# First chunks of every fold taken out of the rank-2 projection and put into w2

## The chip, the cores and the metric

One core of a Trainium2 chip runs the kernel. The metric is the device time in microseconds of one execution; the median of three runs before the change is 841.76 us (841.53 to 842.29). The engines are named as the profile names them: PE (matmul), DVE (VectorE), ACT (ScalarE), POOL (GpSimd) and SP, which issues the DMAs.

## What is computed

The input x has 2 x 2048 rows of 1024. Each row is normalised (xn); g is a gated feed-forward network with rank-2 additions to its three weights, and s an aggregation over lags of the row's autocorrelation:

```python
def _qlora_linear(x, wq, A, B):
    w = jnp.tile(wq, (1, 4))
    return x @ w.T + (x @ A.T @ B.T) * 0.5

xn = _layernorm(x)
s  = _L0_attn_ref(xn)              # sum over the 6 strongest lags, softmax weights
gate = silu(_qlora_linear(xn, w1q, a1, b1))
up   = _qlora_linear(xn, w3q, a3, b3)
g  = silu(_qlora_linear(gate * up, w2q, a2, b2))
return x + s * g
```

The weights are tiled four times along their inputs, so products with them are taken of a folded input: four quarters are added first. With gate * up = h (2752 wide), the last product is fold(h) @ w2q.T plus half of (h @ a2.T) @ b2.T, where a2 is 2 x 2752.

## The kernel before

The 4096 rows are taken in eight **token groups** of 512 (i = 0 to 7). In a token group the 2752 hidden columns are taken as 22 **pairs** p (a gate and an up matmul chain each, `up(i, p)`), ordered so that pairs 4n to 4n+3 are the four quarters of fold chunk n (n = 0 to 4), and pairs 20 and 21 hold what is left over, the rests. An even pair is a chain of six matmuls for gate and six for up, an odd one begins with `lora` (four matmuls of 32 rows that close the pair before and open this one). ACT makes silu of gate (`gate`), DVE multiplies with up (`product`, into one of six slots of h) and adds the quarters of a fold (`add_chunk`). Each folded chunk is split into a high part (ACT, `folded_high`) and a low part (DVE, `folded_low`, tile hf_l), and `down` multiplies both with w2, itself split into w2_h (ACT, `w2_high`) and w2_l (DVE, `w2_low`, `w2_tail`). In token group 0 `down` is split into `down_high` and `down_low`, since w2_l is still being made.

The rank-2 projection of h by a2 is `z2`: a **batch** is four pairs, each a matmul that gives 6 rows of 512 in a strip of the bank zb. `Z2_AT` says after which pair a batch stands, and the last one stands in the down projection. For fold chunks 3 and 4 (`BASE`) the first quarter is in no batch: a2 of the quarter is subtracted from that of the three others (POOL, `a2_diff`), and its outer product with b2, halved, is added to w2 by DVE, two rank-1 steps `add_base` per chunk with the rows of b2 broadcast by DMA (base_b). So 20 of 22 pairs stand in five batches. In the tail, `tail_shifts` (ACT) and `tail_sums` (DVE) move and add the strips of pairs 20 and 21.

Token group 0 has work that the others don't have: the split of the weights (`w_high`, `w_low`, with w_low ahead of the first chain of a weight block at pairs 4, 10 and 16), of b (`b_step`), of w2, and the x of token group 1 is transposed (`second_x`, four of its eight behind pairs 14 to 17; the first of those waits until `lag_gap` on DVE has reduced the bank mb). POOL computes the inverse deviations (`spread`) and the sums and differences of xn (`sums`: yh, xq, dd) of the next token group, four tiles per group. The order of each engine's work is written by hand: tables such as `BASE_AT`, `W2_AT`, `NORM_AT` and `STATS_AT` name the pair after which a step stands. DMAs are all issued by SP in the order of its program.

## Time and profile before

| what | value |
|---|---|
| median of three runs | 841.76 us |
| the profiled execution | 841.59 us |
| its span, first to last instruction | 839.8 us |
| PE busy | 821.7 us (98%) |
| DVE busy | 583.8 us (70%) |
| ACT busy | 331.6 us (39%) |
| POOL busy | 148.4 us (18%) |
| granted TensorE clock | full in all 40 slices |
| chain that ended last | PE 87%, DVE 5%, ACT 3% |

Matmuls overlap in the trace: each is shown with its whole duration, and the next starts before it has ended; the distance of two starts is what one costs. The shares are means over stages that differ: DVE's 70% is 97% from 47 to 74 us and less in the token groups behind.

### The profile page before, as it was taken

The page shows a single profiled execution, that of the slowest core. Times are in us where ns is not written, and L with a number is a line of the kernel's source. Part 1 is how long each engine was busy: PE and PEld are TensorE (multiplying, and loading weights), DVE is VectorE, ACT ScalarE, POOL GpSimd, SP SyncE. Part 2 cuts the span into 40 slices and gives each one's busy share as a digit, 9 for nine tenths or more (in the row PEclk, how much of TensorE's full clock was granted, in tenths as well). Part 3 has the DMA queues.
Part 4 walks back from the last instruction along what each step waited for, and adds up shares of the span by engine and source line. Part 5 has one row for each costly group of instructions (what it writes and reads, how often), then busy time and mean ns, then how long its engine had stood idle before and what let it go on. Part 6 is the DMA issues. An engine that isn't in the chain of part 4 may idle for free.

```text
span 839.8 us, 11191 instructions
## 1 busy us (share of the span) xinstructions
PE 821.7 (98%) x4168; PEld 438.9 (52%) x4168; DVE 583.8 (70%) x947; ACT 331.6 (39%) x544; POOL 148.4 (18%) x242
## 2 busy tenths in 40 slices
PE   5999999999999999999999999999999999999997
PEld 4444575345844367434763347534585345844366
DVE  7889844686766876688667785678776696744535
ACT  5986644434133342333423432333423434132231
POOL 5324102222012220122102230023201222000000
PEclk9999999999999999999999999999999999999999
DMA  9832035000230003300051010501015000220004
GB/s 286 291 96 76 26 123 204 26 26 25 102 126 26 26 26 126 101 26 26 27 176 50 26 51 2 201 25 51 26 52 176 26 0 1 101 101 1 0 2 151
DMA packets 19191, 63.18 MB, mean 75 GB/s; under 512 B 2496, under 2 KB 4256, under 8 KB 18864
## 3 DMA queue, kind: packets, MB, share of 16 engines
q1 hardware_dynamic: 19120, 62.33, 21.6%
q8 instruction: 33, 0.54, 0.3%
q14 instruction: 38, 0.31, 0.1%
HBM read 45.54 MB, written 16.78 MB: 74 GB/s over the span
## 4 chain that ended last, share of the span: by engine, by line
PE 87%; DVE 5%; ACT 3%; issue 2%; DVEq 2%; DMA 1%; SPq 0%; POOL 0%; ACTq 0%; POOLq 0%
PE g L1290 26%; PE u L1290 23%; PE g L1508 4%; PE u L1508 4%; PE zb L1449 4%; PE u L1517 4%; PE g L1517 4%; PE u L1515 4%; PE g L1515 4%; PE g L1341 3%; ACT w_sq L567 1%; PE mb L1378 1%; DMA xf<-in_x 1%; PE g L1511 1%; PE u L1511 1%
## 5 line engine op out<-in xcount | busy, mean ns | idle before, releaser
L567 ACT ACTIVATE sil<-g,winv 128x512 f32<-128x512 f32 (+1 forms) x176 | 119.9, 683 | 269.2 <-PE g L1341 240.3
L889 DVE SCALAR_TENSOR_TENSOR h<-u,winv,sil 128x512 f32<-128x512 f32 x168 | 125.6, 749 | 113.0 <-ACT sil L567 97.6
L1290 PE MATMUL g<-xt,w_h 128*128 128x512 f16 x656 | 196.2, 381 | 0.0
L1290 PE MATMUL u<-xt,w_h 128*128 128x512 f16 x656 | 195.1, 379 | 0.0
L832 DVE CUSTOM_DVE_ANT_0 junk<-xn,abc 128x1024 bf16<-128x1024 f32 x96 | 120.3, 1253 | 6.0 <-issue 2.7
L1290 PE MATMUL u<-xt,w_l 128*128 128x512 f16 x328 | 124.3, 379 | 0.0
L1290 PE MATMUL g<-xt,w_l 128*128 128x512 f16 x328 | 124.3, 379 | 0.0
L1290 PEld LDWEIGHTS u<-xt,w_h 128*128 128x128 f16 x656 | 64.2, 98 | 77.4
L1290 PEld LDWEIGHTS g<-xt,w_h 128*128 128x128 f16 x656 | 55.4, 98 | 83.9 <-issue 33.3
L464 POOL TENSOR_TENSOR ve<-mv,three 128x1 f32<-128x1 f32 x30 | 6.2, 207 | 471.7 <-DVE mv L814 471.7
L1040 DVE SCALAR_TENSOR_TENSOR ob<-xr,c_mean,gg 128x1024 f32<-128x1024 f32 x27 | 34.6, 1283 | 58.1 <-ACT gg L567 35.4
L567 ACT ACTIVATE gg<-g 128x512 f32<-128x512 f32 x32 | 19.1, 598 | 140.5 <-PE g L1511 65.9
L1508 PE MATMUL g<-w_h,hf_h 128*128 128x512 f32 x174 | 71.6, 411 | 1.4 <-ACT gg L567 1.4
L1508 PE MATMUL u<-w_h,hf_h 128*128 128x512 f32 x174 | 69.0, 397 | 0.0
L1517 PE MATMUL u<-w_h,hf_l 128*128 128x512 f32 x145 | 57.5, 397 | 0.0
L1517 PE MATMUL g<-w_h,hf_l 128*128 128x512 f32 x145 | 57.4, 396 | 0.0
L1515 PE MATMUL u<-w_l,hf_h 128*128 128x512 f32 x145 | 57.4, 396 | 0.0
L1515 PE MATMUL g<-w_l,hf_h 128*128 128x512 f32 x145 | 57.4, 396 | 0.0
L901 DVE TENSOR_TENSOR acc<-acc,h 128x512 f32<-128x512 f32 x80 | 57.1, 714 | 0.0
L1290 PEld LDWEIGHTS g<-xt,w_l 128*128 128x128 f16 x328 | 32.1, 98 | 38.7
L1290 PEld LDWEIGHTS u<-xt,w_l 128*128 128x128 f16 x328 | 32.1, 98 | 38.7
L511 POOL TENSOR_TENSOR yh<-xn 128x512 f32<-128x512 f32 x28 | 37.1, 1324 | 46.9 <-ACT xn L567 46.9
(258 smaller groups left out, 1138.2 us busy)
## 6 DMA issues: line engine op xcount, KB each, us to landing
xr<-in_x SPq DMA_DIRECT2D x32, 512.0 KB, 4.6
out_x<-ob SPq DMA_DIRECT2D x31, 512.0 KB, 2.9
xf<-in_x SPq DMA_DIRECT2D x30, 512.0 KB, 3.3
raw_w<-in_w2t SPq DMA_DIRECT2D x1, 2560.0 KB
abc<-in_a SPq DMA_DIRECT2D x1, 2048.0 KB, 8.1
raw_w<-in_w1t SPq DMA_DIRECT2D x2, 768.0 KB, 8.4
raw_w<-in_w3t SPq DMA_DIRECT2D x2, 768.0 KB, 9.8
base_b<-in_w2t SPq DMA_DIRECT2D x2, 512.0 KB, 4.8
```

Of the source, the lines that this page charges most:

```text
L511: tt(yh[:], xn[:, 0:HALF], xn[:, HALF:L], ALU.add).then_inc(sum_done, 1)
L567: return nc.scalar.activation(out, in_, f, **kw)
L832: nc.vector.tensor_tensor_reduce(junk[:], xn[:], abc[:, r, :], 1.0, 0.0, ALU.mult, ALU.add, zt[:, q, r:r + 1]).then_inc(z_done, 1)
L889: stt(out=h[0:n, p % NH, :], in0=up, scalar=winv[0:n, 3 * block_of(p) + 1:3 * block_of(p) + 2], in1=sil[0:n, p % 2, :], op0=ALU.mult, op1= ...
L901: o = tt(acc[0:rows, b, :], a, h[0:rows, p % NH, :], ALU.add)
L1040: stt(out=o[:], in0=x[:], scalar=c_mean[:, q:q + 1], in1=gg[:], op0=ALU.subtract, op1=ALU.mult)
L1290: o = mm(bank[:], a, x, start=opens and t == 0, stop=closes and t == len(terms) - 1)
L1341: o = mm((gb, ub)[s % 2][k % 3][:], bst[32 * s:32 * s + 32, p // 2, :], zst[32 * s:32 * s + 32, :], start=s >= 2 and not first, stop=s < 2 ...
L1449: o = mm(zb[c:c + 6, :], a2st[:, p, :], h[:, p % NH, :], start=n == 0, stop=n == ZB - 1)
L1508: mm(bank[:], hf_h[:, n, t], w2_h[:, n, c:c + 512], start=n == 0, stop=False)
L1515: mm(bank[:], hf_h[:, n, t], w2_l[:, n, c:c + 512], start=False, stop=False)
L1517: mm(bank[:], hf_l[:, n, t], w2_h[:, n, c:c + 512], start=False, stop=False)
```

## The change

All five fold chunks, and the rests, now have their first part in w2. In the rests pair 20 and the strip of pair 21 are brought together in one projection (`JOINT`): a copy by ACT puts the upper half of pair 21 over the lower rows of pair 20's slot. 16 pairs are left, in four batches, at other pairs of the order. The first rank-1 step per chunk of w2 is now a multiplication by ACT (`base_share`, two buffers share0 and share1) and an addition by POOL (`add_share`); the second stays with DVE (`add_base`), six instead of two, with a row of b2 of its own (base_b1). `w2_high` waits for it in all six chunks.

```diff
-BASE = (3, 4)
-Z_PAIRS = tuple(p for p in range(NP_) if p not in [4 * n for n in BASE])
+NBASE = HN + 1
+JOINT = 4 * HN
+Z_PAIRS = tuple(p for p in range(JOINT) if p % 4) + (JOINT,)
...
-        W2L_AT = {19: 0, 20: 1}
...
-        BASE_AT = {10: (0, 0), 12: (1, 0), 17: (0, 1), 18: (1, 1)}
-        Z2_AT = {5: 0, 9: 1, 13: 2, 19: 3}
+        SHARE_AT = {8: 0, 9: 1, 12: 2, 13: 3, 15: 4, 17: 5}
+        SHARE_BEHIND = ((0,), (), (3, 4), (5,))
+        BASE_AT = {10: 0, 16: 1, 17: 2, 18: 3, 19: 4, 20: 5}
+        C_LOADS = 13
+        Z2_AT = {7: 0, 12: 1, 17: 2}
...
-        W2_AT = {13: 0, 15: 1, 16: 2, 19: 3, 20: 4, 21: 5}
+        W2_AT = {13: 0, 17: 1, 18: 2, 19: 3, 20: 4, 21: 5}
...
+                    if i == 0:
+                        sp.wait_ge(b_rest_done, 4)
+                        sp.dma_start(base_b1[:], d["w2t"][97, HN, :].partition_broadcast(P)).then_inc(base1_loaded, 16)
                     front_load(i + 1, 3)
...
+            def add_share(n):
+                pool.wait_ge(w2_loaded, 16 * 7)
+                pool.wait_ge(share_done, n + 1)
+                tt(raw_w2[:, n, :], raw_w2[:, n, :], share[n % 2][:], ALU.add).then_inc(share_added, 1)
...
                     if i + 1 < NG:
                         spread(i + 1, q)
+                        if i == 0 and q in (1, 2):
+                            add_share(q)
                         sums(i + 1, q)
+                        if i == 0:
+                            for n in SHARE_BEHIND[q]:
+                                add_share(n)
...
-                A(half_b[0:32, :], h[32:64, LAST % NH, :], ACT.Copy).then_inc(shift_done, 1)
-                act.wait_ge(half_done, at_group(i, 2, 2))
+                act.wait_ge(half_done, at_group(i, 2, 1))
+                A(h[0:32, JOINT % NH, :], h[32:64, LAST % NH, :], ACT.Copy).then_inc(shift_done, 1)
                 A(half_b[0:32, :], half_a[32:64, :], ACT.Copy).then_inc(shift_done, 1)
+
+            def base_share(n):
+                act.wait_ge(base_loaded, 16)
+                act.wait_ge(base_halved, HN + 1)
+                if n >= 2:
+                    act.wait_ge(share_added, n - 1)
+                A(share[n % 2][:], base_b[:], ACT.Copy, scale=base_a[:, n, 0:1]).then_inc(share_done, 1)
...
-                if n in BASE:
-                    act.wait_ge(base_done, 2 + BASE.index(n) + 1)
+                act.wait_ge(base_done, n + 1)
...
+            def add_base(n):
+                dve.wait_ge(share_added, n + 1)
+                dve.wait_ge(base1_loaded, 16)
+                stt(out=raw_w2[:, n, :], in0=base_b1[:], scalar=base_a[:, n, 1:2], in1=raw_w2[:, n, :],
                     op0=ALU.mult, op1=ALU.add).then_inc(base_done, 1)
...
-                        if p == 9:
+                        if p == 6:
                             half_base()
...
+                if n == ZB - 1:
+                    pe.wait_ge(shift_done, at_group(i, 3, 2))
...
                 if i == 0:
-                    down_high(0, range(0, 3))
+                    down_high(0, range(0, HN))
                     z2(0, ZB - 1)
                     xt_across(1)
                     second_scale()
-                    down_high(0, range(3, HN))
                     down_high(1, range(0, HN))
...
-                    down(i, 0, range(0, 3))
+                    down(i, 0, range(0, 4))
                     z2(i, ZB - 1)
```

The load of a2 by SP, one DMA before, is eleven now, since rows of pairs 20 and 21 change places. `half_base` halves six rows of a2 and one of them twice, in seven instructions instead of two.

POOL in token group 0, from the sums of the second tile to the start of the fourth (raw_w2 is w2, share0 and share1 are ACT's products); before:

```order
L515 TENSOR_TENSOR dd_74<-xn_69 128x256
L464 TENSOR_TENSOR ve_100<-mv_99,three_101 128x1
L465 TENSOR_TENSOR nm_103<-mv_99,three_101 128x1
L467 TENSOR_TENSOR rs_102<-ve_100,three_101 128x1
L469 TENSOR_TENSOR nm_103<-nm_103,rs_102 128x1
L511 TENSOR_TENSOR yh_72<-xn_69 128x512
L513 TENSOR_TENSOR xq4_73<-yh_72 128x256
```

and after, the same stretch:

```order
L537 TENSOR_TENSOR dd_74<-xn_69 128x256
L522 TENSOR_TENSOR raw_w2_139<-raw_w2_139,share0_156 128x1024
L481 TENSOR_TENSOR ve_100<-mv_99,three_101 128x1
L482 TENSOR_TENSOR nm_103<-mv_99,three_101 128x1
L484 TENSOR_TENSOR rs_102<-ve_100,three_101 128x1
L486 TENSOR_TENSOR nm_103<-nm_103,rs_102 128x1
L522 TENSOR_TENSOR raw_w2_139<-raw_w2_139,share1_157 128x1024
L533 TENSOR_TENSOR yh_72<-xn_69 128x512
L535 TENSOR_TENSOR xq4_73<-yh_72 128x256
```

An addition of 1024 columns stands behind or ahead of each tile's sums, six in all.

ACT in token group 0, from the last transposed x of pair 17 to the end of the pairs (w2_h is made by w2_high, xn by the normalisation, hf_h by folded_high); before:

```order
L567 ACTIVATE xT1_149<-mb 128x4x128
L567 ACTIVATE xn_69<-xf1_66,nm_103,rs_102 128x1024
L567 ACTIVATE hf_h_81<-acc_85 128x512
L567 ACTIVATE sil_84<-g0,winv_93 128x512
L567 ACTIVATE sil_84<-g1,winv_93 128x512
L567 ACTIVATE w2_h_55<-raw_w2_139 128x1024
L567 ACTIVATE sil_84<-g2,winv_93 128x512
L567 ACTIVATE w2_h_55<-raw_w2_139 128x1024
L567 ACTIVATE dd_74,far_75<-dd_74 128x256
```

and after:

```order
L595 ACTIVATE xT1_149<-mb 128x4x128
L595 ACTIVATE share1_157<-base_b_117,base_a_116 128x1024
L595 ACTIVATE w2_h_55<-raw_w2_139 128x1024
L595 ACTIVATE xn_69<-xf1_66,nm_103,rs_102 128x1024
L595 ACTIVATE hf_h_81<-acc_85 128x512
L595 ACTIVATE sil_84<-g0,winv_93 128x512
L595 ACTIVATE w2_h_55<-raw_w2_139 128x1024
L595 ACTIVATE sil_84<-g1,winv_93 128x512
L595 ACTIVATE w2_h_55<-raw_w2_139 128x1024
L595 ACTIVATE sil_84<-g2,winv_93 128x512
L595 ACTIVATE w2_h_55<-raw_w2_139 128x1024
```

The sixth share and a w2_high stand ahead of the normalisation, and every silu of pairs 18 to 20 has a w2_high behind it.

DVE in the tail of token group 0, from the last full chunk's hf_l to zc (w_l is made by w2_low, the last w_l by w2_tail); before:

```order
L924 TENSOR_TENSOR hf_l<-acc,hf_h 128x512
L937 TENSOR_SCALAR some<-mb 128x1
L1135 TENSOR_TENSOR w_l<-raw_w_139,w_h 128x1024
L910 TENSOR_TENSOR half_a<-half_a,h 64x512
L913 TENSOR_TENSOR acc<-half_b,h 32x512
L1135 TENSOR_TENSOR w_l<-raw_w_139,w_h 128x1024
L918 TENSOR_TENSOR acc<-half_b,half_a 32x512
L1135 TENSOR_TENSOR w_l<-raw_w_139,w_h 128x1024
L924 TENSOR_TENSOR hf_h<-acc,hf_h 64x512
L1135 TENSOR_TENSOR w_l<-raw_w_139,w_h 64x1024
L1141 SCALAR_TENSOR_TENSOR w_l<-b_hi,low,raw_b_137 64x1024
L929 SCALAR_TENSOR_TENSOR z2f<-zb,zq 64x512
```

and after, from the second w2_low on:

```order
L1169 TENSOR_TENSOR w_l<-raw_w_139,w_h 128x1024
L958 TENSOR_TENSOR hf_h<-acc,hf_h 64x512
L1169 TENSOR_TENSOR w_l<-raw_w_139,w_h 128x1024
L963 SCALAR_TENSOR_TENSOR z2f<-zb,zq 64x512
L966 SCALAR_TENSOR_TENSOR hf_l<-zh_161,low,z2f 64x512
L1192 TENSOR_TENSOR xt<-g,xt 128x512
L1192 TENSOR_TENSOR xt<-u,xt 128x512
L1169 TENSOR_TENSOR w_l<-raw_w_139,w_h 128x1024 x2
L1169 TENSOR_TENSOR w_l<-raw_w_139,w_h 64x1024
L1175 SCALAR_TENSOR_TENSOR w_l<-b_hi,low,raw_b_137 64x1024
L976 TENSOR_TENSOR zc_150<-mb,rsb 128x512
```

All six w2_low stand behind the pairs now, where four did; three of them and w2_tail stand behind the two xt.

## Rows read from the trace of the kernel before

**Rows 1.** The page's first section: engine, busy us, share of the span, instructions.

```profile
PE 821.7 (98%) x4168; PEld 438.9 (52%) x4168; DVE 583.8 (70%) x947; ACT 331.6 (39%) x544; POOL 148.4 (18%) x242
```

**Rows 2.** PE's waits behind token group 0: total us, times, longest us.

```profile
PE g L1508 <- ACT gg L567: 1.4, 1, 1.4
```

**Rows 3.** Timeline of PE in token group 0: start, us, engine, line, instruction [idle before].

```profile
41.43 0.18 PE L1546 MATMUL mb<-wsum,ones_h 128*128 128x2 bf16 x1
...
58.16 0.39 PE L1341 MATMUL g<-zst,bst 32*128 32x512 bf16 x1
...
73.17 0.63 PE L1407 MATMUL mb<-ident,xf 128*128 128x128 f32 x4 [1.76 <-DVE gp L871]
```

**Rows 4.** Timeline of DVE, the product of pair 8 and half_base.

```profile
57.35 0.75 DVE L889 SCALAR_TENSOR_TENSOR h<-u,winv,sil 128x512 f32<-128x512 f32 x1
...
59.27 0.22 DVE L857 TENSOR_SCALAR base_a<-raw_a 128x2 f32<-128x2 f32 x2
```

**Rows 5.** Busy us by stretch: length, PE, PEld, DVE, ACT, POOL, clock, DMA, GB/s.

```profile
74.00:98.00 24.00, 24.00 (x134) 11.55 (x130) 19.76 (x30) 15.65 (x25) 4.22 (x8) 1.00 0.15 52
```

**Rows 6.** Timeline of PE around a batch of token group 1 (two passes of four).

```profile
148.01 0.59 PE L1290 MATMUL u<-xt,w_h 128*128 128x512 f16 x2
148.44 0.38 PE L1290 MATMUL u<-xt,w_l 128*128 128x512 f16 x1
148.75 1.04 PE L1449 MATMUL zb<-h,a2st 128*6 128x512 f32 x8
149.73 0.60 PE L1378 MATMUL mb<-xt,fwd 128*128 128x512 f16 x2
```

**Rows 7.** Timeline of ACT in token group 0: last square of the weights, w2_high(0).

```profile
41.18 0.20 ACT L567 ACTIVATION_READ_ACCUMULATOR w_sq<-raw_w 128x1 bf16 x1
...
69.04 1.04 ACT L567 ACTIVATE w_h<-raw_w 128x1024 fp32r<-128x1024 f32 x1
```

**Rows 8.** Timeline of ACT and PE in the tail of token group 7.

```profile
803.43 0.63 ACT L567 ACTIVATE half_a<-h 64x512 f32<-64x512 f32 x1
...
806.17 1.04 PE L1449 MATMUL zb<-h,a2st 128*6 128x512 f32 x8
```

**Rows 9.** SP's own waits up to 130 us: total us, times, longest us.

```profile
SPq L373 <- POOL dd L500: 8.3, 2, 8.1
```

**Rows 10.** Timeline of SP, the first loads of token group 1.

```profile
28.32 1.01 SPq L373 DMA_DIRECT2D xf<-in_x  x2
```

**Rows 11.** Instructions by line: ns min/median/max, first and last start, forms.

```profile
L511 POOL TENSOR_TENSOR yh<-xn x28: 1267/1277/2105, 46.2 to 703.1; 128x512 f32<-128x512 f32 x28
...
L515 POOL TENSOR_TENSOR dd<-xn x28: 721/1172/1707, 48.2 to 705.6; 128x256 f32<-128x256 f32 x28
...
L924 DVE TENSOR_TENSOR hf_l<-acc,hf_h x40: 675/686/1758, 51.1 to 803.5; 128x512 fp32r<-128x512 f32 x40
...
L889 DVE SCALAR_TENSOR_TENSOR h<-u,winv,sil x168: 735/750/753, 29.7 to 801.4; 128x512 f32<-128x512 f32 x168
```

**Rows 12.** Timeline of DVE and POOL from 62.3 to 65 us.

```profile
62.38 1.29 DVE L865 SCALAR_TENSOR_TENSOR raw_w<-base_b,base_a,raw_w 128x1024 f32<-128x1024 f32 x1
...
62.69 2.10 POOL L511 TENSOR_TENSOR yh<-xn 128x512 f32<-128x512 f32 x1 [3.94 <-ACT xn L567]
...
63.58 1.76 DVE L924 TENSOR_TENSOR hf_l<-acc,hf_h 128x512 fp32r<-128x512 f32 x1
```

**Rows 13.** Timeline of PE and DVE, down projection of token group 0.

```profile
94.41 0.58 PE L1463 MATMUL g<-w_h,hf_h 128*128 128x512 f32 x1
...
97.49 0.69 DVE L924 TENSOR_TENSOR hf_l<-acc,hf_h 128x512 fp32r<-128x512 f32 x1
...
98.29 1.21 DVE L1135 TENSOR_TENSOR w_l<-raw_w,w_h 128x1024 fp32r<-128x1024 f32 x1
...
98.47 0.66 PE L1539 MATMUL g<-ident,xq 128*128 128x128 f32 x4
...
110.80 0.39 PE L1479 MATMUL g<-w_h,hf_h 128*128 128x512 f32 x1
```

More of the change, by code:

```diff
@@ L238, in build @@
         b_part = sb("b_part", [P, NP_ // 2, P], BF16, at=o_at + 4096)
+        base_b1 = sb("base_b1", [P, L], F32, at=o_at + 4096)
+        share = [sb("share0", [P, L], F32, at=gg_at), sb("share1", [P, L], F32, at=hf_at + 8192)]
         w_sq = sb("w_sq", [P, 2, 768], BF16, at=gg_at)
@@ L418, in _ @@
                     block_load(b, m)
-            for buf, name in ((raw_a2, "a2t"), (fwd, "fwd"), (inv, "inv")):
+            a2 = d["a2t"]
+            sp.dma_start(raw_a2[:, 0:JOINT, :], a2[:, 0:JOINT, :]).then_inc(c_loaded, 16)
+            sp.dma_start(raw_a2[32:P, JOINT, :], a2[32:P, JOINT, :]).then_inc(c_loaded, 16)
+            sp.dma_start(raw_a2[0:32, JOINT, :], a2[32:64, LAST, :]).then_inc(c_loaded, 16)
+            sp.dma_start(raw_a2[0:32, LAST, :], a2[0:32, LAST, :]).then_inc(c_loaded, 16)
+            for rows in (32, 64, 96):
+                sp.dma_start(raw_a2[rows:rows + 32, LAST, :], a2[0:32, JOINT, :]).then_inc(c_loaded, 16)
+            for rows in (0, 64):
+                for part in range(2):
+                    sp.dma_start(base_a[rows + 32 * part:rows + 32 * part + 32, HN, :],
+                                 a2[0:32, JOINT + part, :]).then_inc(c_loaded, 16)
+            for buf, name in ((fwd, "fwd"), (inv, "inv")):
                 sp.dma_start(buf[:], d[name]).then_inc(c_loaded, 16)
@@ L543, in _ @@
                 raw_difference(q)
-            pool.wait_ge(c_loaded, 16 * 3)
-            for n in BASE:
+            pool.wait_ge(c_loaded, 16 * C_LOADS)
+            for n in range(HN):
                 tt(raw_a2[:, 4 * n + 1:4 * n + 4, :], raw_a2[:, 4 * n + 1:4 * n + 4, :],
                    raw_a2[:, 4 * n:4 * n + 1, :].broadcast_to([P, 3, 2]), ALU.subtract).then_inc(a2_diff, 1)
-            pool.wait_ge(a2_diff, len(BASE))
+            tt(raw_a2[:, JOINT, :], raw_a2[:, JOINT, :], raw_a2[:, LAST, :], ALU.subtract).then_inc(a2_diff, 1)
+            pool.wait_ge(a2_diff, NBASE)
             for u in range(3):
@@ L769, in _ @@
                             b_cast(CAST_AT[p])
+                        if p in SHARE_AT:
+                            base_share(SHARE_AT[p])
                         if p in W2_AT:
@@ L854, in half_base @@
             def half_base():
[L855 to L865 removed]
+                dve.wait_ge(c_loaded, 16 * C_LOADS)
+                for n in range(HN):
+                    ts(base_a[:, n, :], raw_a2[:, 4 * n, :], 0.5, None, ALU.mult).then_inc(base_halved, 1)
+                ts(base_a[:, HN, :], base_a[:, HN, :], 0.5, None, ALU.mult).then_inc(base_halved, 1)
+            def add_base(n):
+                dve.wait_ge(share_added, n + 1)
+                dve.wait_ge(base1_loaded, 16)
+                stt(out=raw_w2[:, n, :], in0=base_b1[:], scalar=base_a[:, n, 1:2], in1=raw_w2[:, n, :],
                     op0=ALU.mult, op1=ALU.add).then_inc(base_done, 1)
@@ L1211, in _ @@
                             w_low(b, m, k)
-                        if p == 9:
+                        if p == 6:
                             half_base()
                         if p in BASE_AT:
-                            add_base(*BASE_AT[p])
-                        if p in W2L_AT:
-                            w2_low(W2L_AT[p])
+                            add_base(BASE_AT[p])
                     if not last and p in STATS_AT[i]:
@@ L1230, in _ @@
                     flag(0)
-                    w2_low(2)
                 tail_sums(i)
                 if i == 0:
-                    w2_low(4)
+                    w2_low(1)
                 folded_low(i, HN)
                 if i == 0:
-                    w2_low(HN)
-                    w2_tail()
+                    w2_low(2)
                     dve.wait_ge(zeroed, 10)
@@ L1243, in _ @@
                     xt_low(i + 1, 1)
+                if i == 0:
+                    w2_low(3)
+                    w2_low(4)
+                    w2_low(HN)
+                    w2_tail()
                 if i == 0:
@@ L1624, in _ @@
                         xt_across(i + 1)
-                    down(i, 0, range(3, HN))
+                    down(i, 0, range(4, HN))
                     down(i, 1, range(0, HN))
```

32 lines of the change are left out of this document (10 added, 22 removed).

## Prediction

> **What bounds the kernel now.** I read the page's busy line first: PE works 821.7 of 839.8 us [rows 1], so a microsecond taken from PE in a steady token group is a microsecond off the kernel, as long as nobody makes PE wait in its place. The second view is therefore the list of PE's waits and the timeline behind it. From token group 1 on PE waits once, 1.4 us for ScalarE in a down projection [rows 2]. In token group 0 it waits 1.76 us in front of the transposes behind pair 14 (73.17), for VectorE's reduction of the lags [rows 3]; and already at pair 11 there is no margin: the product of pair 8 ends at 57.35 + 0.75 = 58.10 [rows 4], and the lora matmul that needs its bank starts at 58.16 [rows 3]. The third view, the busy time by stretches, says how much room VectorE has after that: 19.76 of 24.00 us are busy from 74 to 98, so 4.2 us are free [rows 5]. Hence the question of this change: it takes PE work out of every token group, and pays with work of VectorE, ScalarE and GpSimd that lies all in token group 0, where VectorE sets PE's pace.
>
> **The batch that goes.** Two plain matmuls start 0.43 us apart from their successor (148.01 to 148.44), so one takes 0.215. From the last one before a batch (148.44) to the next instruction's start (149.73) it is 1.29 [rows 6]. A batch costs 1.29 - 0.215 = 1.07 us. After pair 12 the batch is now followed by lora's four narrow matmuls, which the trace doesn't show behind a batch; the bounds are 0.98 (148.75 to 149.73 alone) and 1.17 (one more step of about 0.1, as 148.44 to 148.75 shows beyond 0.215). I take 1.07: seven token groups give 7.5 us (6.9 to 8.2). In token group 0 the batch after pair 5 goes, but the scale sum behind it starts at 41.43 [rows 3], right after ScalarE's accumulator read has ended at 41.18 + 0.20 [rows 7]: PE would stand there instead. Nothing is gained in that group.
>
> The last batch now waits for a copy within h. In the last token group ScalarE starts half_a at 803.43; 0.63 for it, 0.68 for VectorE's sum and 0.63 for the copy give 805.4, while PE comes there one chunk of six matmuls (1.4) after 806.17, at 807.6 [rows 8]: hidden, with 2 us to spare. The products of pairs 7 and 17 wait for a batch, but PE asks for their banks three pairs later; free. SP gets ten more small loads ahead of token group 1's x, where it now waits 8.1 us for GpSimd [rows 9]; a load there is issued in 0.5 (two in 1.01 [rows 10]), at twice that ten take 10. I take nothing, and 2.0 us of late x as the end.
>
> **The additions.** GpSimd takes 0.72 for 256 columns and 1.27 for 512 when undisturbed, so about 1.27 + 2 x 0.54 = 2.35 for 1024 (at most 2 x 1.27 = 2.54). What that does to VectorE is in the rows around 63 us: yh was issued at 62.69 while add_base held 62.38 to 63.67, and took 2.10, and VectorE's subtraction, issued at 63.58, took 1.76 where 0.68 is usual and ended 0.55 after yh's end (64.79). An instruction with two operands in SBUF waits out GpSimd's whole instruction, and GpSimd has its turn as soon as it asked first. VectorE's products, with one operand in PSUM, never vary (735 to 753 ns in 168) [rows 11, 12]. The Trainium skill says the same and more sharply (SBUF — State Buffer, section "SBUF: two separate sides"): the shared port pair is an exclusive lock held for the whole instruction; by it 2.35 us are lost whole wherever an addition meets such work, and if the ports were shared instead, about half would be. No run here shows an addition of 1024 columns yet. The skill's GPSIMD Engine Reference, section 4.1, tells one to put elementwise additions on VectorE; six there would cost some 7.2 us of VectorE at 1.2 each, against the 10.8 of waits that I find below.
>
> Followed through token group 0, with the time by which a thing is later than before:
>
> Up to pair 11. half_base is seven small instructions where two fill 0.22 now [rows 4], so 0.5 to 0.8 more; I take 0.5. It stands ahead of pair 7. The first share costs ScalarE what a copy of this size does (1.04 [rows 7]) and ends as b_step runs; from there VectorE has b_step and two w_low, all with two SBUF operands, up to the statistics: the first addition costs it 2.35. The product of pair 8 comes 2.85 later, and since PE had 0.06 to spare, lora(11) too: +2.85.
>
> Up to the transposes behind pair 14. The second addition falls beside products and statistics: 0. The third meets w_low of the last block or an addition of the fold: 2.2. add_base at pair 12 has moved away: -1.2. The reduction and PE behind it: +3.8.
>
> Up to the last full fold's hf_l (97.49 [rows 13]). Fourth addition 1.55 (what is left of it when VectorE comes), fifth 2.3, sixth 2.35; GpSimd's sums of the last tile now fall among add_base and add_chunk: 1.1; five add_base instead of two: 3.6; two w2_low fewer, at 1.21: -2.4; the 4.2 of room used up. ScalarE's in-order queue adds two: the sixth share and w2_high(1), which waits for VectorE, stand ahead of the normalisation and of the silu of pair 18 (2.3), and w2_high(5), which waits for the last add_base, stands ahead of the last folded_high (0.9). Sum 7.5, so hf_l comes at 97.5 + 3.8 + 7.5 = 108.8. PE, held by w_low's last quarter at pair 16 too, stands by then at the fifth chunk of the down projection, which needs it.
>
> The tail. Behind that folded_high ScalarE has b2_high (1.05), half_a (0.63), then VectorE's sum (0.68) and the copy (0.63): the batch starts near 111.7 and the transposes behind it at 112.6. Before, they started at 98.47 with three chunks done; two more chunks, at a third of 98.47 - 94.41 less the batch (1.07) and its changes of shape, 0.94 each, make 100.35: +12.3 [rows 13]. Then all six w2_low stand in VectorE's tail, four of them behind the two xt_low: from the sum's end (110.9) six at 1.21, w2_tail at 1.3 and seven of some 0.68 with 0.6 of waits end at 124.9. PE's way from the transposes to the first matmul that needs w2_tail was 98.47 to 110.80; less the two chunks it is 10.4, so PE asks at 123.0: 1.9 more.
>
> Token group 0: +14.2; the rest -7.5. The profiled execution took 841.59 (span 839.8 and 1.8 around it), 0.02% under the median of 841.76: 841.6 + 14.2 - 7.5 = **848.3 us**. With the loss bounded by 10 (ScalarE's queue and the sums of the last tile cost nothing) and 17 (additions at 2.54, late x) it is 844 to 851.5.
>
> **Rivals.** *GpSimd gives way* (faster): if its additions slip into VectorE's one-operand work and 4.2 us of room, the loop of token group 0 keeps its pace (+0.5), and only the waits of the tail stay (0.3 for hf_l, 1.6 for the copy, 1.9 for w2_tail, by the same steps from 97.49): 841.6 - 7.5 + 4.3 = 838.4. For it: no wait but 1.76 us is seen in that group now. Against it: every meeting of two such instructions in the rows makes one wait. It decides at a loss under 7.5 us in group 0. *Half the meetings* (no change): half of the 10.8 us of additions meets nothing: +8.8, less some of ScalarE's queue, +8.2, so 842.3. *Later still*: SP's loads late by 2.0 and additions at 2.54 (1.1 in all): 851.4. *The batch gives nothing*: if the narrow matmuls behind it hid it already, 855.8; the start times of [rows 6] speak against it.
>
> **How the numbers follow.** Forecast 0.60, later still 0.10, nothing from the batch 0.03, half the meetings 0.12, GpSimd gives way 0.15. A measurement of this kernel can tell 0.2% (1.7 us) from no change: under 840.1 is faster, 0.15; up to 843.4 is the same, 0.12; slower 0.73. The range of 8 in 10 cuts the outer part of the fast case and the last: 839 to 852; the forecast's own is 844 to 851.5.
>
> **What would show it.** Per token group from 1 on, PE's period 1.07 shorter. In group 0: additions of 2.35 us or longer on GpSimd, w_low or add_chunk of over 2 us beside them, lora(11) near 61, the transposes behind pair 14 near 77, the batch of the tail near 112, w2_tail's end near 125 with PE waiting for it. It is wrong if VectorE's two-operand instructions keep their usual length beside the additions, or if PE enters the down projection of group 0 within 3 us of before.

## The result, and the profile after

The changed kernel takes 855.0 us (median of four executions, 854.43 to 855.66) against 842.0 of the kernel before: a ratio of 1.0155, with a 95% interval of 1.0142 to 1.0167. So the sign of the forecast was right and its size wrong: +13 us where +6.7 was forecast, outside the range. The profiled execution has a span of 853.0 (before 839.8). The page's first section, which answers to [rows 1], and the row of granted clocks in 40 slices of 21.3 us:

```profile
PE 820.4 (96%) x4104; PEld 441.6 (52%) x4104; DVE 593.6 (70%) x953; ACT 336.6 (39%) x550; POOL 167.5 (20%) x252
...
PEclk9999889999999999999999999999999999999999
```

PE's busy time falls by 1.3 us only (part of it is spent at a lower clock), and PE now waits 4% of the span; two slices of token group 0 run at a lower clock, which the row of before shows nowhere. PE's longest waits in the whole execution (total us, times, longest us), to be read beside [rows 2]:

```profile
PE zb L1486 <- ACT h L595: 5.6, 7, 0.9
PE mb L1604 <- DVE a_raw L1200: 4.9, 1, 4.9
PE u L1343 <- DVE w_l L1156: 4.4, 3, 2.7
PE g L1500 <- DVE hf_l L958: 2.9, 1, 2.9
```

The first row is new and comes once in token groups 0 to 6: the last batch waits for ScalarE's copy. The second stood in the kernel before too (5.0). The third and fourth lie in token group 0.

The starts of the token groups' pairs on PE (the first matmul of pair 0) divide the loss. Token group 1 starts at 149.33 instead of 131.81: **+17.5** (forecast +14.2). From there to the end it is 703.6 instead of 708.0: **-4.4** (forecast -7.5). The period of token groups 1 to 6 (the distance of two such starts) is 100.13 (before 100.38 to 100.39, once 102.07), and the last group takes 102.9 (before 104.0). Both halves of the forecast are off by 3.1 to 3.3 us, in the same direction.

**Where token groups 1 to 6 lose it.** The tail of token group 1: ScalarE, VectorE, GpSimd and PE, each in order of time (start, duration):

```profile
215.77 1.24 ACT L595 ACTIVATE xn<-xf,nm,rs 128x1024 f32<-128x1024 f32 x1 [2.04 <-POOL nm L486]
216.91 0.67 ACT L595 ACTIVATE sil<-g,winv 64x512 f32<-64x512 f32 x1
...
220.21 0.63 ACT L595 ACTIVATE h<-h 32x512 f32<-32x512 f32 x1 [1.44 <-DVE half_a L944]
...
218.89 1.22 DVE L944 TENSOR_TENSOR half_a<-half_a,h 64x512 f32<-64x512 f32 x1
...
218.46 1.11 POOL L535 TENSOR_TENSOR xq<-yh 128x256 f32<-128x256 f32 x1
...
220.89 1.04 PE L1486 MATMUL zb<-h,a2st 128*6 128x512 f32 x8 [0.87 <-ACT h L595]
```

The normalisation xn of the next token group stands ahead of the silu of pair 21 in ScalarE's queue, and half_a's sum meets GpSimd's xq and takes 1.22. So the copy ends 0.87 after PE wants it. The same place in the last token group, which has no next one:

```profile
815.24 0.69 ACT L595 ACTIVATE sil<-g,winv 64x512 f32<-64x512 f32 x1 [0.72 <-PE g L1325]
...
818.03 0.63 ACT L595 ACTIVATE h<-h 32x512 f32<-32x512 f32 x1 [0.81 <-DVE half_a L944]
...
820.74 1.04 PE L1486 MATMUL zb<-h,a2st 128*6 128x512 f32 x8
```

Here the copy has ended two us before PE comes. The prediction took its timing from this group ([rows 8]).

**Where token group 0 loses it.** VectorE and GpSimd around 80 us; L1152 and L1156 are the four pieces of w_low's last two quarters, L522 is the addition:

```profile
79.71 0.59 DVE L1152 SCALAR_TENSOR_TENSOR wp_l<-raw_w,wscl,wp_h 128x64 f16<-128x64 f32 x1
80.22 2.99 DVE L1156 SCALAR_TENSOR_TENSOR w_l<-raw_w,wscl,w_h 128x640 f16<-128x640 f32 x1
83.14 2.36 DVE L1152 SCALAR_TENSOR_TENSOR wp_l<-raw_w,wscl,wp_h 128x64 f16<-128x64 f32 x1
85.42 0.87 DVE L1156 SCALAR_TENSOR_TENSOR w_l<-raw_w,wscl,w_h 128x640 f16<-128x640 f32 x1
...
80.18 5.24 POOL L522 TENSOR_TENSOR raw_w<-raw_w,share 128x1024 f32<-128x1024 f32 x2
```

The fourth and fifth addition run back to back, and each takes its turn between two pieces of w_low: from 79.71 to 86.29 it is 6.6 us for what takes 2.4 with one-column additions (adds_short below). PE waits 1.15 and 2.69 inside pair 16 for it. And then PE itself is slow. Busy us by stretch (length, PE, PEld, DVE, ACT, POOL, granted clock, DMA, GB/s):

```profile
64.10:84.50 20.40, 17.95 (x99) 7.84 (x97) 18.36 (x22) 14.67 (x23) 15.18 (x13) 1.00 0.16 52
84.70:91.30 6.60, 4.95 (x17) 2.11 (x18) 6.38 (x11) 1.80 (x5) 1.88 (x5) 0.50 0.00 0
91.40:111.80 20.40, 16.67 (x84) 7.96 (x82) 14.49 (x14) 11.87 (x17) 6.43 (x4) 1.00 0.07 27
112.00:118.60 6.60, 5.60 (x20) 2.98 (x21) 5.55 (x8) 4.32 (x7) 0.00 (x0) 0.50 0.00 1
```

The granted clock is 0.50 (1.2 instead of 2.4 GHz) in two stretches of 6.8 us, from 84.6 and from 111.9 on (and in one of 3.4 from 60.7). Each of the two begins inside a wait, the first inside that of 2.69 (1.15 came shortly before it), the second inside that of 2.90 (1.67 before it).

### The profile page after: what moved, and what is told of

Its sections match the earlier page's. It is cut to its first block, busy times and chain, and to the rows that moved or that the text cites. A ratio compares the mean times of both kernels' runs of the same rounds, so it can differ in the third digit from the quotient of the medians.

```text
span 853.0 us, 11125 instructions
## 1 busy us (share of the span) xinstructions
PE 820.4 (96%) x4104; PEld 441.6 (52%) x4104; DVE 593.6 (70%) x953; ACT 336.6 (39%) x550; POOL 167.5 (20%) x252
## 4 chain that ended last, share of the span: by engine, by line
PE 78%; DVE 7%; ACT 5%; DVEq 4%; issue 3%; POOL 2%; DMA 1%; SPq 0%; ACTq 0%; POOLq 0%
PE g L1325 22%; PE u L1325 21%; PE g L1545 4%; PE u L1545 4%; PE zb L1486 4%; PE u L1554 3%; PE g L1554 3%; PE u L1552 3%; PE g L1552 3%; PE g L1376 3%; DVEq L939 3%; DVE h L923 1%; ACT sil L595 1%; ACT w_sq L595 1%; DVE half_a L944 1%
## 5 line engine op out<-in xcount | busy, mean ns | idle before, releaser
L923 DVE SCALAR_TENSOR_TENSOR h<-u,winv,sil 128x512 f32<-128x512 f32 x168 | 125.5, 748 | 112.1 <-ACT sil L595 95.6
```

The costliest lines, as they stand in the source:

```text
L923: stt(out=h[0:n, p % NH, :], in0=up, scalar=winv[0:n, 3 * block_of(p) + 1:3 * block_of(p) + 2], in1=sil[0:n, p % 2, :], op0=ALU.mult, op1= ...
```

## The experiments

All are edits of the changed kernel; the start of token group 1 (149.33 there) is given as t1. It is counted from the first instruction, and token group 0 itself starts at 19.6 to 22.0 us in the thirteen profiles (19.67 in the changed kernel, 19.73 before), so a difference of 1 us in t1 can lie ahead of the work of token group 0.

**The tail of the steady groups.** z2_late:

```diff
-                    down(i, 0, range(0, 4))
+                    down(i, 0, range(0, HN))
                     z2(i, ZB - 1)
                     if not last:
                         xt_across(i + 1)
-                    down(i, 0, range(4, HN))
```

> The changed kernel with one move on PE: in token groups 1 to 7 the last batch (and the transposes behind it) stands behind the fifth chunk of the down projection, not behind the fourth. Theory A: in groups 1 to 6 PE waits 0.87 us each for ScalarE's copy within h, because there the next group's normalisation stands ahead of the silu of pair 21 and because half_a's sum meets GpSimd's sums (1.22 instead of 0.68); one chunk of six matmuls (1.4 us) covers that, and nothing behind it comes late. Then the period of groups 1 to 6 falls from 100.13 to 99.3 and the time from 855.0 by 5.2 to 849.8. Rival B: a batch less is worth little whatever happens in the tail, and the wait returns further on (at the corner chunk, which needs what is made of zb, or at the next group's x): period 100.1, time 854 to 855.

Measured: 848.06 us. In the profile the batch doesn't wait any more, and the period falls from 100.13 to 99.6, not to 99.3:

```profile
219.07 1.04 PE L1486 MATMUL zb<-h,a2st 128*6 128x512 f32 x8
...
238.16 0.50 PE L1545 MATMUL g<-w_h,hf_h 128*128 128x512 f32 x1 [0.15 <-ACT gg L595]
```

About 0.3 of the 0.87 come back at the fourth tile, whose banks ScalarE hasn't read (the step up to this matmul is 0.55 from start to start where 0.24 is usual; 0.15 of it shows as idle): the next wait in line, as rival B said, but only a third of it. From t1 on the profile is 2.9 us shorter. The other 2.3 of its 5.2 lie in token group 0 (t1 = 147.05), where nothing was edited; that is taken up under changed_again.

**The additions and the rank-1 steps, left out.** adds_short, base_short, both_short:

```diff
-                tt(raw_w2[:, n, :], raw_w2[:, n, :], share[n % 2][:], ALU.add).then_inc(share_added, 1)
+                tt(raw_w2[:, n, 0:1], raw_w2[:, n, 0:1], share[n % 2][:, 0:1], ALU.add).then_inc(share_added, 1)
...
-                stt(out=raw_w2[:, n, :], in0=base_b1[:], scalar=base_a[:, n, 1:2], in1=raw_w2[:, n, :],
+                stt(out=raw_w2[:, n, 0:1], in0=base_b1[:, 0:1], scalar=base_a[:, n, 1:2], in1=raw_w2[:, n, 0:1],
```

The first edit alone is adds_short, the second alone base_short.

> The changed kernel with GpSimd's six additions of 1024 columns cut to one column each, all waits kept; the first rank-1 step is so left out of w2 but for one column. Theory A (the lock): VectorE's instructions with two operands in SBUF are longer than usual beside the additions by 1.8 (w_low, 54 us), 1.1 and 0.6 (hf_l and an addition, 66 to 69), 1.6 (72), 4.2 (w_low, 80 to 86) and 2.2 (hf_l, 102), 11.5 us in all; without them PE is not starved at 83 and 86 us either, so that its granted clock stays at full, worth another 2 to 4 us. Token group 1 then starts at 134 to 139 instead of 149.3, and the time is 840 to 845. Rival B (the work, not the meeting): VectorE's six add_base and ScalarE's queue make the loss; then 851 to 854.

Measured: 842.97 us, t1 = 137.20. The same pieces of w_low as above, now beside GpSimd's small sums only:

```profile
76.21 0.59 DVE L1152 SCALAR_TENSOR_TENSOR wp_l<-raw_w,wscl,wp_h 128x64 f16<-128x64 f32 x1
76.73 0.87 DVE L1156 SCALAR_TENSOR_TENSOR w_l<-raw_w,wscl,w_h 128x640 f16<-128x640 f32 x1
77.53 0.27 DVE L1152 SCALAR_TENSOR_TENSOR wp_l<-raw_w,wscl,wp_h 128x64 f16<-128x64 f32 x1
77.72 0.87 DVE L1156 SCALAR_TENSOR_TENSOR w_l<-raw_w,wscl,w_h 128x640 f16<-128x640 f32 x1
```

The additions cost 12.0 us (12.1 in t1): theory A. By VectorE's durations in both profiles it is w_low 2.1 (4.04 against 1.94 at 54 us) and 4.2 (at 80), an addition of the fold 1.55 (2.23 against 0.68) and hf_l 2.16 (2.84 against 0.68): 10.0. The hf_l and the addition at 66 to 68 us, which the expectation counted too, are as long without them (1.77 and 1.23): those meet GpSimd's sums, as before.

> The changed kernel with VectorE's six add_base cut to one column, GpSimd's additions and all waits kept; the second rank-1 step is so left out of w2 but for one column. Theory A (the lock sets group 0): of 7.7 us of VectorE's work only what lies on the path goes, the one behind the sixth addition and the one ahead of the last w2_high, about 1.3 each, and some of the queue around 100 us: 850 to 853. Rival B (VectorE's work sets group 0): 855.0 - 7.7 = 847, or less.

Measured: 850.01 us, t1 = 144.57, at the end of theory A: 7.7 us of VectorE's work cost 5.0 (4.8 in t1). Not all of it is work: VectorE is ahead from the first add_base on (the piece of w_low at 70.79 stands at 69.28), and so the third addition, at 70.77, holds up only a small step of the lags (0.90 instead of 0.17) where it had cost 1.55.

> The changed kernel with GpSimd's six additions and VectorE's six add_base all cut to one column, all waits, ScalarE's shares and the order kept; both rank-1 steps are so left out of w2 but for one column. Theory A (the two losses add up): the additions were worth 12.1 us of the start of token group 1 (149.3 to 137.2), the add_base 4.8 (149.3 to 144.6); together 132.4, and 838 us. Rival B (they overlap: once the meetings are gone, add_base lies in VectorE's free time): 136 to 137, and 842 to 843. What is left above the 131.8 of before is then due to ScalarE's queue, half_base, the waits of the tail and PE's clock.

Measured: 839.56 us, t1 = 134.54: between the two. Together they are worth 14.8, not 16.9, so 2.1 of the two losses are the same microseconds. What is left above 131.81 is 2.7, with 1.2 of it a wait of the last batch for the copy and 1.6 one for w2_tail; the granted clock is 1.00 from 22 us on.

**Where the additions run.** adds_on_vector moves them to VectorE, one pair behind each share:

```diff
-        SHARE_BEHIND = ((0,), (), (3, 4), (5,))
+        ADD_AT = {9: 0, 10: 1, 13: 2, 14: 3, 16: 4, 18: 5}
...
-            def add_share(n):
-                pool.wait_ge(w2_loaded, 16 * 7)
...
+            def add_share(n):
+                dve.wait_ge(w2_loaded, 16 * 7)
```

> The changed kernel with the six additions made by VectorE, one pair behind each share, instead of GpSimd; the same sums are computed. VectorE gets six times 1.21 = 7.3 us of work and loses the meetings. Theory A (the lock, 11.5 us): 855.0 - 11.5 + 7.3 = 850.8, or less by 1 to 3 where PE's clock no longer falls: 848 to 851. Rival B (VectorE's work is what counts, GpSimd's additions lie beside it): 855 + 7 less what fits into its idle time, 858 to 862.

Measured: 850.60 us, t1 = 145.29, as theory A has it: the same sums, 7.3 us more work on the engine that sets the pace, and 4.4 us less time. The prediction's comparison (7.2 against 10.8) came out. The Trainium skill (GPSIMD Engine Reference, section 4.1) tells one to put elementwise additions on VectorE; this run agrees.

**The clock.** filled_waits gives PE matmuls without use where it waits:

```diff
                 def lower(k):
+                    if p == BLOCK[3] and m == 1:
+                        pe.wait_ge(mult_done, at_pair(0, p - 2))
+                        for _ in range((5, 12)[k]):
+                            mm(gb[(p + 1) % 3][:], wt_h[0][:, 0, c:c + P], xt[:, 0, :], start=True, stop=True)
                     pe.wait_ge(wl_done, 4 * b + 2 * m + k + 1)
...
                 for n in ns:
+                    if q == 0 and n == HN - 1:
+                        pe.wait_ge(mult_done, at_pair(0, NP_ - 2))
+                        for _ in range(11):
+                            mm(gb[DN[1]][:], hf_h[:, 0, t], w2_h[:, 0, 0:512], start=True, stop=True)
```

> The changed kernel; PE gets 28 matmuls whose results nobody reads, at places where it waits in token group 0: 5 and 12 in the up chain of pair 16, each ahead of a wait for a quarter of w_low, and 11 ahead of the fifth chunk of the down projection. Theory A (the clock): in the changed kernel PE ran at half the granted clock from 84.6 to 91.4 and from 111.9 to 118.7 us; what it had to do there with nothing to wait for took some 5 and 3.6 us, so 2.5 and 1.8 us were lost. With PE busy the granted clock stays at 1.00 there and the time falls by 2 to 4 us, to 851 to 853. Rival B (PE waits for VectorE and ScalarE a little later anyway): the clock stays up and the time doesn't move by more than 1 us: 854 to 856.

Measured: 852.79 us, t1 = 147.47. The two stretches that ran at half the clock, in this kernel:

```profile
84.70:91.30 6.60, 6.50 (x39) 2.63 (x37) 6.38 (x10) 2.15 (x5) 2.07 (x4) 1.00 0.00 0
112.00:118.60 6.60, 5.37 (x33) 3.93 (x34) 6.40 (x8) 4.47 (x8) 0.00 (x0) 1.00 0.01 1
```

PE kept its clock in both, and 2.2 us came back for 28 matmuls that compute nothing. That is less than this kernel's single times can differ by (changed_again), but the two profiles show where it comes from: the fifth chunk starts at 110.78 instead of 112.63, and from there to t1 it is 36.69 instead of 36.70. So the first stretch is on the path, with 1.9 of t1, and the second isn't, for what PE gains there it waits for later:

```profile
113.23 1.04 PE L1490 MATMUL zb<-h,a2st 128*6 128x512 f32 x8 [1.25 <-ACT h L595]
...
126.40 0.47 PE L1524 MATMUL g<-w_h,hf_h 128*128 128x512 f32 x1 [1.60 <-DVE w_l L1175]
```

In the changed kernel the first of these waits was 0.37 and the second didn't occur. Of the 4.3 that the expectation counts for the halved clock, half came back.

**ScalarE's order.** queue_order:

```diff
-        W2_AT = {13: 0, 17: 1, 18: 2, 19: 3, 20: 4, 21: 5}
+        W2_AT = {13: 0, 17: 1, 18: 2, 19: 3}
...
+                    if i == 0 and p == LAST:
+                        act.wait_ge(share_added, NBASE)
                     if p % 4 == 1 and p > 1:
                         folded_high(i, p // 4 - 1)
                     if i == 0 and p == LAST:
-                        b2_high()
+                        w2_high(HN - 1)
...
                 A(zh2[:], z2f[:], ACT.Copy).then_inc(zh2_done, 1)
+                if i == 0:
+                    w2_high(HN)
+                    b2_high()
```

> The changed kernel with another order on ScalarE alone: w2_high of the fifth chunk stands behind folded_high of the fifth chunk, and w2_high of the rests and b2_high stand behind the copies of the batch, instead of ahead of folded_high and of the tail's copies. Theory A (ScalarE's order sets the end of token group 0): hf_l comes 0.9 earlier, and the copy for which the batch waits another 1.05 (b2_high) and up to 1.06 earlier: 852 to 853. Rival B (VectorE is as late as ScalarE: its sixth add_base ends at 110.16, and w2_tail, for which PE asks at 128, now comes later): 854.5 to 856.

Measured: 849.12 us, t1 = 144.09. More than theory A allowed: of the 5.2 in t1, 2.3 are those that z2_late shows in token group 0 without any edit there (the two profiles show the same course at 80 us, see changed_again), which leaves some 3 for the order. Token group 0 starts 2.3 later here than in the changed kernel, though; counted from its own start it is 7.5 shorter, and in z2_late 3.1, which would leave 4.4, and the median times leave 1.8. So the order's share is positive, and its size isn't pinned down.

**Is it the same course each time?** In z2_late and queue_order w_low at 80 us is not hit as above (the course above is called the first here, this one the second). In z2_late the fourth addition ran alone, at 78.85, and met an addition of the fold (1.50 where 0.92 stood); the pieces of w_low behind it kept their usual length:

```profile
80.26 1.50 DVE L935 TENSOR_TENSOR acc<-h 128x512 f32<-128x512 f32 x1
81.83 0.29 DVE L1152 SCALAR_TENSOR_TENSOR wp_l<-raw_w,wscl,wp_h 128x64 f16<-128x64 f32 x1
82.03 0.88 DVE L1156 SCALAR_TENSOR_TENSOR w_l<-raw_w,wscl,w_h 128x640 f16<-128x640 f32 x1
```

changed_again is the changed kernel, unedited.

> The changed kernel once more, nothing altered. In its first profile GpSimd's fourth and fifth addition ran back to back from 80.2 to 85.4 us and met three of the four pieces of w_low, so that PE waited 3.8 us inside pair 16; in z2_late, queue_order and filled_waits, whose order is the same up to there on all engines, the fourth addition met one addition of the fold instead and PE waited 0.5 us or less at that place, though token group 0 started some 0.8 us later. Theory A (which instruction a given addition meets is decided by a few hundred ns of the loads at the start, and varies from execution to execution): the new profile may show either course, and the times of this kernel spread over 2 us or more, 851 to 856. Rival B (the course belongs to the kernel): the same course again, 854.4 to 855.7.

Measured: 854.80 us, with single times from 850.35 to 857.38; the profile shows the first course again (5.24 us of two additions from 80.05). The expectation was wrong on filled_waits, which has the first course too (5.23 from 80.71) and only covers PE's wait. So there are five profiles whose instructions are the same up to there. In the three of the first course the granted clock was 0.50 for 3.4 us from 60.5 to 61.1 on; in the two of the second it was 1.00 until 76 us. The two go together, and the traces show the path between them, up to the third addition. The waits of 0.54 and 1.76 us ahead of 61 us are the same in all five. Where the clock is 0.50 behind them, PE ends pair 12 later, ScalarE's silu of it comes later, and so do the third share behind it and the third addition, for which GpSimd waits 0.85. In the changed kernel:

```profile
69.71 0.69 ACT L595 ACTIVATE sil<-g,winv 128x512 f32<-128x512 f32 x1 [1.75 <-PE g L1376]
70.30 1.14 ACT L595 ACTIVATE share<-base_b,base_a 128x1024 f32<-128x1024 f32 x1
...
71.57 2.36 POOL L522 TENSOR_TENSOR raw_w<-raw_w,share 128x1024 f32<-128x1024 f32 x1 [0.85 <-ACT share L595]
```

and in z2_late:

```profile
71.45 2.40 POOL L522 TENSOR_TENSOR raw_w<-raw_w,share 128x1024 f32<-128x1024 f32 x1
...
71.56 2.98 DVE L1156 SCALAR_TENSOR_TENSOR w_l<-raw_w,wscl,w_h 128x640 f16<-128x640 f32 x1
...
77.20 1.09 PE L1442 MATMUL mb<-ident,xf 128*128 128x128 f32 x4 [2.65 <-DVE gp L905]
```

From the first addition to the third it is 17.4 to 17.5 us in the three and 16.6 in the two, while the piece of w_low begins 16.7 behind the first addition in all five. So in the second course the third addition meets that piece (2.98 instead of 0.88), PE waits 2.65 at the transposes behind pair 14 instead of 0.5, and the wait inside pair 16 is gone. A full clock alone doesn't spare pair 16: in base_short, with the clock at 1.00 from 22 to 83 us, the third addition misses w_low as well, the next two meet it at 78.5, and PE waits 1.79 and 2.69. No run was made that sets the clock at 60 us alone, so that this is what spreads the times over 7 us (theory A), with a profile that repeats (rival B), is likely, not shown.

**A version that beats both.** two_steps lets VectorE make both rank-1 steps, with no shares and no additions elsewhere, and keeps z2_late and queue_order:

```diff
-        SHARE_AT = {8: 0, 9: 1, 12: 2, 13: 3, 15: 4, 17: 5}
-        SHARE_BEHIND = ((0,), (), (3, 4), (5,))
-        BASE_AT = {10: 0, 16: 1, 17: 2, 18: 3, 19: 4, 20: 5}
+        BASE_AT = {10: ((0, 0),), 12: ((0, 1),), 15: ((1, 0),), 16: ((1, 1),), 17: ((2, 0), (2, 1)),
+                   18: ((3, 0),), 19: ((3, 1),), 20: ((4, 0), (4, 1))}
...
-                stt(out=raw_w2[:, n, :], in0=base_b1[:], scalar=base_a[:, n, 1:2], in1=raw_w2[:, n, :],
-                    op0=ALU.mult, op1=ALU.add).then_inc(base_done, 1)
+                stt(out=raw_w2[:, n, :], in0=(base_b, base_b1)[row][:], scalar=base_a[:, n, row:row + 1],
+                    in1=raw_w2[:, n, :], op0=ALU.mult, op1=ALU.add).then_inc((share_added, base_done)[row], 1)
```

> A version meant to beat both: as the changed kernel in what is computed, with both rank-1 steps made by VectorE (twelve of 1.28 us, no shares on ScalarE, no additions on GpSimd), those of the rests in the tail; the last batch behind the fifth chunk in token groups 1 to 7, and behind two chunks of the second tile in token group 0; w2_high of the fifth chunk behind folded_high, that of the rests and b2_high behind the batch's copies, all w2_low at the end of VectorE's tail. Theory A (meetings and waits made the loss): VectorE has 15.4 of add_base where it had 5.1, and up to pair 21 two w2_low fewer (2.4) and 4.2 us of room, so the loop of token group 0 gets 2 to 5 us longer; the periods fall to 99.6; 838 to 843. Rival B (VectorE's work in token group 0 costs what it takes): 10.3 more there, 842 + 10.3 - 6.9 = 845 or more.

Measured: 846.91 us, t1 = 144.00. PE enters the down projection at 96.36 (before 94.41, [rows 13]), as theory A has it, but then waits 2.3 for hf_l, 1.9 for w2_low and 1.8 for w2_tail, and runs at half the clock from 74.9 to 78.3 and from 119.3 to 126.1. The loop was mended; the tail took it back, as rival B's sum has it. three_tiles puts PE's other work into these waits:

```diff
-                    down_high(0, range(0, HN))
-                    down_high(1, range(0, 2))
+                    down_high(0, range(0, HN - 1))
+                    down_high(1, range(0, HN - 1))
                     z2(0, ZB - 1)
                     xt_across(1)
                     second_scale()
-                    down_high(1, range(2, HN))
+                    down_high(0, range(HN - 1, HN))
+                    down_high(1, range(HN - 1, HN))
                     second_z0()
+                    pe.wait_ge(xtl_done, 4)
+                    down_high(2, range(0, HN))
                     down_low(0)
```

> two_steps with other work put into PE's waits at the end of token group 0 and less ahead of them on VectorE: both rank-1 steps of the fifth chunk move behind the last pair; the fifth chunk of the first two tiles stands behind the batch; the high part of the third tile stands ahead of all low parts (which need w2_low); add_base at pair 12 moves to pair 15. Theory A (in two_steps PE lost 2.3 for hf_l, 3.7 for w_low and w2_tail and some 3 to a halved clock behind these waits, 9 us between pair 21 and the third tile, and the work of PE can be put there): 4 to 8 us less than 846.9, 839 to 843, and granted clock 1.00 from 90 us on. Rival B (VectorE ends its tail when it ends it, and the third tile's work is then missing as cover for the copies at the start of token group 1): 845 to 848.

Measured: 841.75 us, ratio to before 0.9999 (0.9987 to 1.0012), t1 = 139.09: theory A's size, with waits left of 2.05 for w2_high of the fourth chunk, 0.5 for xt_low, 0.9 for w2_tail and 2.4 for the reading of the second tile's banks, and half the clock from 99.3 to 102.7. early_spread covers those in the same manner:

```diff
+                    down_high(0, range(0, 3))
+                    down_high(1, range(0, 3))
+                    xt_across(1)
+                    down_high(0, range(3, 4))
+                    down_high(1, range(3, 4))
                     z2(0, ZB - 1)
...
                     down_high(2, range(0, HN))
+                    second_spread()
+                    for ns in (range(0, 2), range(2, 3), range(3, 4), range(4, HN)):
+                        for q in range(3):
+                            down_low(q, ns)
+                    for q in range(3):
+                        down_corner(q)
```

> three_tiles with its remaining waits at the end of token group 0 covered: the transposes of the next x ahead of the fourth chunk, the fourth chunk (whose w2_high comes late) behind three chunks of two tiles, second_spread ahead of the low parts, the low parts chunk by chunk over three tiles with the corner behind, the fourth tile in the banks of the first, w2_low of the first five ahead of and between the second tile's start values on VectorE. Theory A (those waits, 2.05 for w2_high, 0.5, 0.9, 2.4 for the reading of the second tile's banks, and 1.7 of a halved clock, are PE time that other work can take): the start of token group 1 moves from 139.1 to 132 to 134 and the time from 841.75 to 835 to 837, faster than both kernels. Rival B (VectorE's chain up to its first output, 15 us behind w2_tail's start, is what ends group 0, and PE only waits elsewhere): 839 to 842.

Measured: **835.95 us**, ratio to before 0.9919 (0.9906 to 0.9933), with t1 = 131.92, a period of 99.6 to 99.7 (100.97 in token group 1, where PE waits 1.29 for its first banks) and the granted clock at 1.00 from 21.4 us on. Busy by stretch, token group 0 and the next (columns as above):

```profile
24.00:132.00 108.00, 104.96 (x561) 57.84 (x560) 89.50 (x130) 73.69 (x116) 28.39 (x44) 1.00 0.32 110
132.00:232.00 100.00, 98.54 (x492) 52.71 (x492) 72.15 (x121) 38.82 (x63) 19.73 (x28) 1.00 0.23 78
```

So token group 0 ends where it ended before (it takes 110.9 from its own start, before 112.1), with all the work of the change in it, and the batch less in every other group is left as gain: 4.8 in groups 1 to 6 (1.7 of it the wait of [rows 2], which is gone) and 1.2 in the last.

## Why the prediction was wrong, step by step

**The batch's price** was right. 100.39 - 100.13 + 0.87 gives 1.13 per group (taken: 1.07, bounds 0.98 to 1.17), and the last group, which has no wait, gains 1.15. *The batch gives nothing*, whose 855.8 lies next to the result, is not what happened: the gain was there, and a wait took it.

**"Hidden, with 2 us to spare"** is the step that failed: the copy ahead of the last batch. Its working was right for the place that it looked at; the last token group does have those 2 us. But that group is the only one in which nothing of a next group is in ScalarE's queue. It costs 0.87 in six groups, 5.2 in all. The 1.4 us wait of [rows 2] was also gone, which the sum didn't foresee (1.7 in the period): -4.4 in place of -7.5, so that a part of the error was covered by luck. The kernel before would have told: in its trace half_a's sum takes 1.224 at the median of the eight token groups and 0.674 at the least, and in its steady tails a normalisation stands ahead of the last silu. Its token group 1:

```profile
198.21 1.24 ACT L567 ACTIVATE xn<-xf,nm,rs 128x1024 f32<-128x1024 f32 x1 [0.83 <-POOL nm L469]
199.36 0.67 ACT L567 ACTIVATE sil<-g,winv 64x512 f32<-64x512 f32 x1
...
201.34 1.23 DVE L910 TENSOR_TENSOR half_a<-half_a,h 64x512 f32<-64x512 f32 x1
...
202.21 1.04 PE L1449 MATMUL zb<-h,a2st 128*6 128x512 f32 x8
```

With the prediction's own numbers the copy would end here at 201.34 + 1.23 + 0.63 = 203.2, while PE, with a chunk more (1.4) and a batch less (1.07) ahead of it, would come at 202.5: PE 0.7 too early, against a measured wait of 0.87.

**Up to pair 11**: forecast lora(11) at 61.0, measured 60.63. **Up to the transposes behind pair 14**: 77.0 and 75.88. The reason given is right and the sizes were a little large: w_low at 54 us lost 2.1 to the first addition (2.35 in the sum), an addition of the fold 1.55 to the third (2.2), and half_base is six instructions that take 0.28 more than before, not seven that take 0.5 more.

**The additions' price** as a whole was right: 10.8 in the sum, 10.0 by VectorE's durations. An addition that meets nothing takes 2.36 (estimated 2.35).

**"The 4.2 of room used up"** is the second step that failed, on the way to the last full fold's hf_l: its start was forecast at 108.8 and came at 111.88, though the transposes behind pair 14 had come 1.1 early. From those transposes to hf_l, before and after (busy us as above):

```profile
73.17:97.49 24.32, 24.32 (x130) 11.93 (x130) 20.01 (x31) 15.14 (x25) 5.05 (x9) 1.00 0.19 61
75.88:111.88 36.00, 28.35 (x134) 13.30 (x134) 28.06 (x32) 18.66 (x29) 15.93 (x13) 0.91 0.08 30
```

VectorE's busy time grew by 8.05, where the sum's terms for its work come to 8.5: that part was right. But its idle time, which the sum let fall by 4.2 and then raised by 3.2 for ScalarE's queue, rose from 4.3 to 7.9. Two of VectorE's waits in this stretch:

```profile
93.67 0.75 DVE L923 SCALAR_TENSOR_TENSOR h<-u,winv,sil 128x512 f32<-128x512 f32 x1 [1.34 <-PE zb L1486]
...
99.01 0.75 DVE L923 SCALAR_TENSOR_TENSOR h<-u,winv,sil 128x512 f32<-128x512 f32 x1 [3.40 <-ACT sil L595]
```

The first is the product of pair 17, whose wait for a batch the prediction called free, because PE asks for its bank later; VectorE stands all the same. The second is the silu of pair 18, behind ScalarE's queue, which in turn waits for PE's transposes behind pair 17. PE has no term in the sum: it was taken to run at full speed behind each wait, and ran at half. With the waits filled (filled_waits) the first of the two is gone, the second is 2.45, and VectorE's idle time in this stretch is 5.6. So 2.4 of the surplus go with PE's clock, and the rest is room that VectorE could not use while ScalarE and PE were late.

**The tail**: the batch forecast near 111.7 came at 115.08, 3.1 of it the lateness of hf_l. w2_tail ended at 128.11 instead of 124.9, and PE asked at 128.26: the 1.9 forecast for it was not there, since PE was as late as VectorE.

**Token group 0** in all: +17.5 for +14.2, of which the clock is some 2 (1.9 in t1, 2.2 in the time). **GpSimd gives way** and **Half the meetings** are both refuted: five of the six additions met work with two operands in SBUF, and cost VectorE 10.0 of the 11.8 us that five of 2.36 last, and without them (adds_short) 12.0 us are gone.

## What to carry to other kernels

A margin that is read in the last pass of a loop holds for the last pass: the steady ones have the next pass's work in every queue, so time a new wait there. A free stretch on one engine can be used only if the engines that feed it are not late as well. Where PE is starved, allow for the time in which it may run slower afterwards, and put other PE work into the wait rather than nothing. And when work is moved off the critical engine onto one that shares its operand path, compare it with leaving it there: here 7.3 us more on VectorE were 4.4 us cheaper than the same sums on GpSimd, and the change paid only once the waits at the end of the first group had been filled.

## What the runs showed of the hardware

**TensorE's clock falls behind short waits.** With waits of 1.15 and 2.69 us, or 1.67 and 2.90, within a few us of each other, the granted clock went to 0.50 for 6.8 us, and with a single one of 2.05 (three_tiles) for 3.4; in the kernel before one wait of 1.76 ([rows 3]) had no such effect. The same two waits, 0.54 and 1.76 us ahead of 61 us, came with 3.4 us of half clock in three profiles (the changed kernel, changed_again, filled_waits) and with none in three others (z2_late, queue_order, base_short): the length of a wait alone doesn't tell. A matmul of 512 columns then takes 0.43 from start to start where it takes 0.22 to 0.23. Work without use in the waits kept the clock at 1.00. The Trainium skill (TensorE: Matmul & The Clock Gate, section "What's actually happening") describes it in this way: the slow clock is the default, and activity of the array releases it. The runs agree: filled waits kept the clock, unfilled ones lost it. A kernel in which PE is 96% busy still paid some 2 us for it.

**Two engines taking turns.** Two additions back to back on GpSimd and four pieces of w_low on VectorE alternated, so that a 64-column piece that takes 0.27 took 2.36: the piece issued at 80.22 ended 0.69 behind the fourth addition's end (82.53), and the fifth addition, issued at 82.48, waited for that piece and took 2.93 instead of 2.36. The rule cited in the prediction (SBUF — State Buffer of the Trainium skill, "SBUF: two separate sides"), that the loser waits for the whole instruction, holds for 1024 columns too. Whether a given addition meets such a piece changed between profiles whose instructions are the same up to there.
